# Destination one-hots of a step by two operations of a tensor with a tensor in place of eight with a per-partition scalar

## The chip, the cores and the metric

The kernel runs on one core of one Trainium2 chip. The metric is the device time of one execution in microseconds (us), the median of the runs shown. Engines: PE is TensorE, DVE is VectorE, ACT is ScalarE, POOL is GpSimd, SP is SyncE.

## What is computed

A graph layer with a residual and a layer norm over 12,500 nodes with 32 features and 200,000 edges, sorted by destination. For each edge from `src` to `dst`:

```python
msg = jnp.concatenate([x_i, x_j - x_i], axis=-1)   # x_i = x[dst], x_j = x[src]
h = relu(msg @ W1 + b1)      # 64 -> 64
h = relu(h @ W2 + b2)        # 64 -> 128
h = relu(h @ W3 + b3)        # 128 -> 64
m = h @ W4 + b4              # 64 -> 32
s = segment_sum(m, dst); cnt = segment_sum(1, dst)
x = layernorm(x + s / maximum(cnt, 1))
```

The edge attributes take no part in it. W4 is applied after the sum over the edges of a node.

## The kernel before

The edges are handled in 196 steps of 1,024 edges (`PT` = 8 tiles of 128). A step comes in one of two kinds, which `STEPS` and `SORTED_AT` lay out by hand: 60 are "sorted" (the rows of the source nodes are selected by matmuls with one-hots that DVE builds) and 136 are "gathered" (the rows are fetched by indirect DMAs that POOL issues). From step 7 to step 188 every third step, at four places every fourth, is a sorted one; the last seven steps are gathered ones.

POOL has one job in the steps: `gather(g)`, whose L585 issues one indirect DMA for each tile of a gathered step, eight to a step, 1,083 in all. They fill a ring `xj` of `R` = 10 steps; `gather` waits (`s_turned`) only if the ring is full.

PE runs the pipeline of a step: the source rows (for a gathered step L919 transposes them out of `xj`; for a sorted one `selected_x`, L964, works in three pieces spread over this and the two preceding steps, and L978 applies layer 1), the destination part of layer 1 (L901), layer 2 (L988), layer 3 (L996), the transposition of its output (`turn_layer3`, L1004), and `sum_window`, which multiplies by the one-hots of the destinations and so sums over the edges (L1016 for a sorted step, 84 nodes wide, L1019 for a gathered one, 42 wide). ACT does the ReLUs.

DVE works through `step(s)` in an order written out by hand. After `copy_x` (L1389) and `copy_layer3(s - 3)` (L1395) come:

- `build_pick(s + 1)`: one comparison of 126x1024 16-bit integers (L1367, for a sorted step L1365, and then `build_wide_pick`, L1371, as a second one);
- `build_onehot(s - 3, tiles)`: for each of the eight tiles one operation of `iota` with a scalar of each partition from `dst_rel` (L1410), float32, 42 columns for a gathered step and 84 for a sorted one, into `onehot`, which is float32 too;
- `hot_of(s, n)`: up to three comparisons of about 128x1500 16-bit integers (`build_hot`, L1380), the one-hots of the sources of the coming sorted steps, eight for each sorted step;
- `add_sums(s - 4)`: adds the sums of a step out of PSUM to `sums` (L1433), one addition for a sorted step and two for a gathered one, each at an offset that is read from memory.

The eight operations of `build_onehot` are made in four pairs with the comparisons between them:

```python
build_pick(s + 1); onehot_free(s - 3)
build_onehot(s - 3, (0, 1))
if next step is sorted: build_wide_pick(s + 1)
build_onehot(s - 3, (2, 3)); hot_of(s, 0)
build_onehot(s - 3, (4, 5)); hot_of(s, 1)
build_onehot(s - 3, (6, 7)); add_sums(s - 4)
hot_of(s, 2)
```

`onehot_free` waits for PE's sum of two steps before, `build_hot` for the landing of its row of sources and, on the first chunk of a piece, for PE; the others of these operations have no wait ahead of them. The steps 3 to 6 (`early_step`) use `build_whole_onehot` (L1418), one operation of a tensor with a tensor for all eight tiles, 336 columns. Before the steps, DVE sorts keys (`merge`: L1290 and L1291, both inputs in SBUF) and splits rows (L1162, both inputs in SBUF), while POOL already issues gathers. After the last step, `messages` (L1081) and the layer norm follow.

Of the kernel before, what the change touches and what calls it, by code (L numbers as in the profile page):

```python
# [9 lines left out]
ALU = mybir.AluOpType  # L10
# [6 lines left out]
P = 128  # L17
# [5 lines left out]
PT = 2 * UT  # L23
PE2 = PT * T
S_N = -(-E // PE2)
# [88 lines left out]
def build(nc, x, src, dst, W1, b1, W2, b2, W3, b3, W4, b4, consts, bounds, out):  # L114
# [3 lines left out]
    with ctx:  # L118
        def sb(name, shape, dt):
            return ctx.enter_context(nc.sbuf_tensor(name, shape, dt))  # L120

        def sem(name):
            return ctx.enter_context(nc.semaphore(name))

        def part(v, first, shape):
            cols = 1
            for n in shape:
                cols *= n
            names = "abcd"[:len(shape)]
            return v[:, first:first + cols].rearrange(  # L130
                f"p ({' '.join(names)}) -> p {' '.join(names)}", **dict(zip(names, shape)))
# [38 lines left out]
        onehot = part(region, 0, (2, PT, WIN))  # L170
# [20 lines left out]
        dst_rel = sb("dst_rel", [P, S_N * PT], F32)  # L191
# [107 lines left out]
        s_pick, s_oh, s_h3c, s_acc = sem("pick_built"), sem("onehot_built"), sem("layer3_copied"), sem("sums_added")  # L299
# [14 lines left out]
        def is_sorted(s):  # L314
            return STEPS[s] < SB
# [788 lines left out]
        def _(dve):  # L1104
# [160 lines left out]
            while size <= PE2:  # L1265
                j = size // 2
# [103 lines left out]
            def build_wide_pick(s):  # L1370
                nc.vector.tensor_scalar(pick[:, s % 2, 1, :], dstb[:, s % RX, :], node_off[0:K3, 2:3], None, ALU.is_equal)\  # L1371
                    .then_inc(s_pick, 1)
# [30 lines left out]
                if s == 0:  # L1403
                    dve.wait_ge(s_dst_st, 2 * 16)

            def build_onehot(s, tiles):
                v, n = s % 2, STEPS[s]
                nodes, w = (iota_s, WIN) if n < SB else (iota_g, KN)
                for j in tiles:
                    last = nc.vector.tensor_scalar(onehot[:, v, j, 0:w], nodes[:, :],  # L1410
                                                   dst_rel[:, n * PT + j:n * PT + j + 1], None, ALU.is_equal)
                if j == PT - 1:
                    last.then_inc(s_oh, 1)

            def build_whole_onehot(s):
                v, n = s % 2, STEPS[s]
# [25 lines left out]
            def hot_of(s, n):  # L1442
                for lead in (1, 2, 3):
                    if s >= AHEAD and s + lead < S_N and is_sorted(s + lead) and n < len(PIECES[3 - lead]):
                        build_hot(STEPS[s + lead], PIECES[3 - lead][n])
# [14 lines left out]
            def step(s):  # L1460
                if s < AHEAD + 3:
                    early_step(s)
                    return
                if s < S_N and is_sorted(s):
                    copy_x(s)
                if s <= S_N + 2:
                    copy_layer3(s - 3)
                if s + 1 < S_N:
                    build_pick(s + 1)
                if s <= S_N + 2:  # L1470
                    onehot_free(s - 3)
                    build_onehot(s - 3, (0, 1))
                if s + 1 < S_N and is_sorted(s + 1):
                    build_wide_pick(s + 1)
                if s <= S_N + 2:
                    build_onehot(s - 3, (2, 3))
                hot_of(s, 0)
                if s <= S_N + 2:
                    build_onehot(s - 3, (4, 5))
                hot_of(s, 1)  # L1480
                if s <= S_N + 2:
                    build_onehot(s - 3, (6, 7))
                add_sums(s - 4)
                hot_of(s, 2)

            build_pick(0)
            for s in range(AHEAD):
# [66 lines left out]
            for n in range(len(CHUNKS) + LAG + 1):  # L1554
                if n > LAG:
                    variance(n - LAG - 1)
                if n < len(CHUNKS):
                    c0, w = CHUNKS[n]
# [44 lines left out]
```

## Time and profile before

| | us |
|---|---|
| median of 3 runs | 1553.71 |
| lowest and highest | 1542.68, 1553.79 |
| the profiled execution, its own time | 1556.37 |
| its span, first to last instruction | 1554.5 |
| busy PE / DVE / ACT / POOL | 1375.3 / 966.0 / 605.6 / 1168.6 |
| mean granted TensorE clock, share of full | 0.937 |

The span is what the rows below are read from; the profiled execution's own time has 1.9 us around it. Instructions of DVE overlap in the records: the next one starts some 0.08 us before the end of the one before it, so the time that one takes in a row of several is the distance from start to start.

### The profile page before, as it was taken

The numbers are of one execution on the slowest core, as the hardware profiler recorded it, in microseconds if no ns is written. First come the engines' busy times: TensorE is split into PE (matmuls) and PEld (weight loads), VectorE is DVE, ScalarE is ACT, GpSimd is POOL, SyncE is SP. The second block draws the span as 40 slices with busy tenths as digits, with TensorE's granted clock in tenths as the row PEclk, the third lists the DMA queues.
The fourth block names the chain that finished last, engine by engine and source line by source line (L and its number), as shares of the span: only waits on it lengthen the run. The fifth ranks groups of instructions, "written<-read, shape, count | busy, mean of one in ns | idle before, by whom it ended". The sixth has DMA issues, their size and how long they took to land.

```text
span 1554.5 us, 40899 instructions
## 1 busy us (share of the span) xinstructions
PE 1375.3 (88%) x14064; PEld 930.6 (60%) x14064; DVE 966.0 (62%) x3159; ACT 605.6 (39%) x952; POOL 1168.6 (75%) x1101
## 2 busy tenths in 40 slices
PE   3254999999999999999989999999899989999676
PEld 2112666666767766766756666666566656766443
DVE  5986566666666666666556666665556655666355
ACT  5354333443343443444333433434324343333323
POOL 4777777777777777777777777777777777777752
PEclk8566999999999999999999999999989998999868
DMA  7538977777767777777667777767657775775411
GB/s 183 163 88 188 296 232 228 220 223 225 226 202 233 232 225 220 224 214 228 185 176 224 209 225 215 213 201 203 196 173 233 209 217 171 233 221 158 105 30 44
DMA packets 197031, 306.55 MB, mean 197 GB/s; under 512 B 84519, under 2 KB 90010, under 8 KB 196257
## 3 DMA queue, kind: packets, MB, share of 16 engines
q1 hardware_dynamic: 161485, 267.17, 56.2%
q0 software_dynamic: 34656, 34.90, 10.5%
q8 instruction: 115, 1.88, 0.5%
q10 hardware_dynamic: 682, 1.85, 0.5%
q14 instruction: 93, 0.75, 0.2%
HBM read 289.68 MB, written 13.92 MB: 195 GB/s over the span
## 4 chain that ended last, share of the span: by engine, by line
POOL 66%; issue 20%; DVE 5%; PE 3%; DMA 3%; SPq 2%; ACT 0%; DVEq 0%; POOLq 0%; ACTq 0%
POOL xj L585 66%; DVE region L1290 1%; DVE region L1291 1%; DMA sums<-in_src 1%; SPq L524 1%; DMA x_rows<-x_p 1%; PE ps L964 1%; DMA xj<-z_rows,src_t 1%; DVE work L1156 0%; PE ps L1019 0%; PE ps L988 0%; DVE work L1162 0%; PE ps L996 0%; DMA region<-src_rows 0%; PE ps L1081 0%
## 5 line engine op out<-in xcount | busy, mean ns | idle before, releaser
L585 POOL DMA_INDIRECT xj<-z_rows,src_t x1043 | 1111.1, 1065 | 317.9 <-issue 317.0
L964 PEld LDWEIGHTS ps<-region,x_p 128*96 128x96 bf16 x6780 | 397.8, 126 | 53.8 <-issue 53.2
L964 PE MATMUL ps<-region,x_p 128*96 128x127 bf16 (+54 forms) x6780 | 418.6, 220 | 8.1 <-DVE region L1380 8.1
L731 ACT ACTIVATE work<-ps,b3s 128x512 f32<-128x512 f32 x196 | 134.7, 687 | 562.7 <-PE ps L996 554.7
L1380 DVE TENSOR_SCALAR region<-region,cst 128x1629 bf16<-128x1629 int16 x480 | 302.1, 630 | 13.3 <-DMA region<-src_rows 13.1
L1395 DVE COPY work<-ps 128x512 f32<-128x512 f32 x195 | 133.9, 687 | 271.2 <-PE ps L1004 268.9
L724 ACT ACTIVATE work<-ps,b2s 128x512 f32<-128x512 f32 x392 | 248.0, 683 | 69.8 <-PE ps L988 69.8
L716 ACT ACTIVATE work<-ps,b1s 128x512 f32<-128x512 f32 x196 | 134.7, 687 | 237.8 <-PE ps L901 237.5
L988 PE MATMUL ps<-work,w2s 64*128 64x512 f32 x784 | 224.9, 651 | 1.0 <-ACT work L716 0.9
L996 PE MATMUL ps<-work,w3s 128*64 128x512 f32 x784 | 213.3, 623 | 0.0
L1410 DVE TENSOR_SCALAR region<-iota_g,dst_rel 128x42 f32<-128x42 f32 x1056 | 206.7, 251 | 0.0
L919 PEld LDWEIGHTS ps<-cst,xj 128*128 128x128 f32 x544 | 60.2, 147 | 185.2 <-issue 185.1
L919 PE MATMUL ps<-cst,xj 128*128 128x128 f32 x544 | 93.3, 297 | 79.3 <-DMA xj<-z_rows,src_t 65.0
L988 PEld LDWEIGHTS ps<-work,w2s 64*128 64x128 f32 x784 | 59.9, 187 | 168.3 <-issue 111.9
L1019 PE MATMUL ps<-region,work 128*65 128x42 f32 x2176 | 156.2, 235 | 1.9 <-DVE sums L1433 1.9
L1019 PEld LDWEIGHTS ps<-region,work 128*65 128x65 f32 x2176 | 154.8, 145 | 3.1 <-issue 3.0
L1389 DVE CAST work<-ps 96x512 bf16<-96x512 f32 x60 | 41.2, 687 | 158.9 <-PE ps L964 153.2
L1433 DVE TENSOR_TENSOR sums<-sums,ps 65x42 f32 (+1 forms) x332 | 65.6, 198 | 108.5 <-DVE sums L1433 97.1
L1004 PE MATMUL ps<-cst,work 128*128 128x128 f32 x784 | 131.6, 292 | 0.0
L1004 PEld LDWEIGHTS ps<-cst,work 128*128 128x128 f32 x784 | 86.0, 146 | 33.9 <-issue 33.1
L1410 DVE TENSOR_SCALAR region<-iota_s,dst_rel 128x84 f32<-128x84 f32 x480 | 101.7, 268 | 0.0
L901 PE MATMUL ps<-region,ywin 126*64 126x512 bf16 x512 | 94.1, 403 | 6.4 <-DVE region L1367 6.4
(156 smaller groups left out, 810.1 us busy)
## 6 DMA issues: line engine op xcount, KB each, us to landing
dstb<-dst_rows SPq DMA_DIRECT2D x196, 252.0 KB
region<-src_rows SPq DMA_DIRECT2D x120, 391.2 KB
region<-src_rows SPq DMA_DIRECT2D x60, 407.2 KB
region<-src_rows SPq DMA_DIRECT2D x60, 403.2 KB
region<-src_rows SPq DMA_DIRECT2D x60, 376.2 KB
region<-src_rows SPq DMA_DIRECT2D x60, 375.8 KB
region<-src_rows SPq DMA_DIRECT2D x60, 374.0 KB
region<-src_rows SPq DMA_DIRECT2D x60, 366.2 KB
```

Of the source, the lines that this page charges most:

```text
L585: pool.indirect_dma_start(out=xj[:, u, j % UT, j // UT, 0:w], out_offset=None, in_=rows, in_offset=bass.IndirectOffsetOnAxis(ap=cols[:, j: ...
L716: nc.scalar.activation(h1[:, v, :], p_h1, ACT.Relu, bias=b1s[:, 0:1]).then_inc(s_r1, 1)
L724: nc.scalar.activation(h2[:, v, h, :], p_h2[:, h, :], ACT.Relu, bias=b2s[:, 0:1]).then_inc(s_r2[h], 1)
L731: nc.scalar.activation(h3[:, v, :], p_h3, ACT.Relu, bias=b3s[:, 0:1]).then_inc(s_r3, 1)
L919: turned = nc.tensor.matmul(to[:, t * T:(t + 1) * T], xj[:, u, t, :, :].rearrange("p h f -> p (h f)"), ident, start=t == 0, stop=True, is_ ...
L964: chosen = nc.tensor.matmul(ps[0:XP, XBANK[h], lo - h * UE:hi - h * UE], xb[:, a, :], hot[:, q % QN, at + lo:at + hi], start=not begun[h], ...
L988: nc.tensor.matmul(p_h2[:, h, :], w2s[r:r + H1, :], h1[r:r + H1, s % 2, :], start=True, stop=True).then_inc(s_l2[h], 1)
L996: nc.tensor.matmul(p_h3[h * H3:(h + 1) * H3, :], w3s[:, :], h2[:, s % 2, h, :], start=True, stop=True).then_inc(s_l3, 1)
L1004: turned = nc.tensor.transpose(p_ht[:, t * T:(t + 1) * T], h3[:, s % 2, t * T:(t + 1) * T], ident)
L1019: summed = nc.tensor.matmul(p_agg[:, h * KN:(h + 1) * KN], h3t[:, v, t, h, :], onehot[:, v, j, 0:KN], start=t == 0, stop=t == UT - 1)
L1380: nc.vector.tensor_scalar(hot[:, q % QN, 0:CW[c]], spread[:, q % QE, 0:CW[c]], cst[:, C_PID:C_PID + 1], None, ALU.is_equal).then_inc(s_hot, 1)
L1410: last = nc.vector.tensor_scalar(onehot[:, v, j, 0:w], nodes[:, :], dst_rel[:, n * PT + j:n * PT + j + 1], None, ALU.is_equal)
```

## The change

`build_onehot` makes half of the tiles of a step in one operation of a tensor with a tensor, in which both inputs are spread by a stride of zero, so that two operations stand in place of eight. Their places among the comparisons change with it.

```diff
-            def build_onehot(s, tiles):
+            def build_onehot(s, j0, j1):
                 v, n = s % 2, STEPS[s]
                 nodes, w = (iota_s, WIN) if n < SB else (iota_g, KN)
-                for j in tiles:
-                    last = nc.vector.tensor_scalar(onehot[:, v, j, 0:w], nodes[:, :],
-                                                   dst_rel[:, n * PT + j:n * PT + j + 1], None, ALU.is_equal)
-                if j == PT - 1:
-                    last.then_inc(s_oh, 1)
+                made = nc.vector.tensor_tensor(onehot[:, v, j0:j1, 0:w],
+                                               nodes[:, :].unsqueeze(1).to_broadcast([P, j1 - j0, w]),
+                                               dst_rel[:, n * PT + j0:n * PT + j1].unsqueeze(2).to_broadcast([P, j1 - j0, w]),
+                                               ALU.is_equal)
+                if j1 == PT:
+                    made.then_inc(s_oh, 1)
...
                 if s <= S_N + 2:
                     onehot_free(s - 3)
-                    build_onehot(s - 3, (0, 1))
+                    build_onehot(s - 3, 0, PT // 2)
                 if s + 1 < S_N and is_sorted(s + 1):
                     build_wide_pick(s + 1)
+                else:
+                    hot_of(s, 0)
                 if s <= S_N + 2:
-                    build_onehot(s - 3, (2, 3))
-                hot_of(s, 0)
-                if s <= S_N + 2:
-                    build_onehot(s - 3, (4, 5))
-                hot_of(s, 1)
-                if s <= S_N + 2:
-                    build_onehot(s - 3, (6, 7))
+                    build_onehot(s - 3, PT // 2, PT)
+                if s + 1 < S_N and is_sorted(s + 1):
+                    hot_of(s, 0)
+                else:
+                    hot_of(s, 1)
                 add_sums(s - 4)
-                hot_of(s, 2)
+                if s + 1 < S_N and is_sorted(s + 1):
+                    hot_of(s, 1)
+                else:
+                    hot_of(s, 2)
```

## Rows read from the trace of the kernel before

**Rows 1.** The page, part 4: the chain of work that ended last, by line.
```profile
POOL xj L585 66%; DVE region L1290 1%; DVE region L1291 1%; DMA sums<-in_src 1%; SPq L524 1%; DMA x_rows<-x_p 1%; PE ps L964 1%; DMA xj<-z_rows,src_t 1%; DVE work L1156 0%; PE ps L1019 0%; PE ps L988 0%; DVE work L1162 0%; PE ps L996 0%; DMA region<-src_rows 0%; PE ps L1081 0%
```
**Rows 2.** Stretches: window, length, then PE, PEld, DVE, ACT, POOL busy (instructions), granted clock, DMA.
```profile
165.00:700.00 535.00, 535.00 (x5792) 368.24 (x5791) 349.38 (x1188) 217.16 (x346) 417.64 (x386) 1.00 0.76 227
700.00:1500.00 800.00, 737.62 (x7583) 504.51 (x7580) 466.71 (x1605) 296.47 (x466) 620.47 (x590) 0.96 0.67 195
```
**Rows 3.** Timeline of POOL, 564 to 575 us: start, length, instruction, idle before.
```profile
564.63 2.39 POOL L585 DMA_INDIRECT xj<-z_rows,src_t  x1 [0.30 <-issue]
567.33 0.94 POOL L585 DMA_INDIRECT xj<-z_rows,src_t  x1 [0.30 <-issue]
...
572.60 1.37 POOL L585 DMA_INDIRECT xj<-z_rows,src_t  x1 [0.30 <-issue]
```
**Rows 4.** Timeline of DVE, the same stretch.
```profile
564.21 0.47 DVE L1367 TENSOR_SCALAR region<-dstb,node_off 126x1024 bf16<-126x1024 int16 x1
564.60 0.78 DVE L1410 TENSOR_SCALAR region<-iota_s,dst_rel 128x84 f32<-128x84 f32 x4
565.31 0.64 DVE L1380 TENSOR_SCALAR region<-region,cst 128x1629 bf16<-128x1629 int16 x1
565.87 0.42 DVE L1410 TENSOR_SCALAR region<-iota_s,dst_rel 128x84 f32<-128x84 f32 x2
566.21 0.60 DVE L1380 TENSOR_SCALAR region<-region,cst 128x1496 bf16<-128x1496 int16 x1
...
567.07 0.19 DVE L1433 TENSOR_TENSOR sums<-sums,ps 65x42 f32 x1
...
572.54 0.60 DVE L1380 TENSOR_SCALAR region<-region,cst 128x1503 bf16<-128x1503 int16 x1
```
**Rows 5.** The chain in order of time: first and last POOL pieces like that at 564.63.
```profile
337.47 2.39 POOL xj L585
...
1358.92 2.39 POOL xj L585
```
**Rows 6.** Timeline of POOL before the steps and in the early ones.
```profile
50.65 2.83 POOL L585 DMA_INDIRECT xj<-in_x,src_t  x1 [0.30 <-issue]
...
163.13 1.17 POOL L585 DMA_INDIRECT xj<-z_rows,src_t  x1 [0.31 <-issue]
```
**Rows 7.** Timeline of DVE, the same stretches.
```profile
50.78 1.21 DVE L1162 TENSOR_TENSOR work<-work 125x1024 bf16<-125x1024 f32 x1
51.92 0.41 DVE L1290 TENSOR_TENSOR region<-region 128x256 f32<-128x256 f32 x1
52.25 0.41 DVE L1291 TENSOR_TENSOR region<-region 128x256 f32<-128x256 f32 x1
...
162.99 0.49 DVE L1418 TENSOR_TENSOR region<-iota_g,dst_rel 128x336 f32<-128x336 f32 x1
163.40 0.18 DVE L1433 TENSOR_TENSOR sums<-sums,ps 65x42 f32 x1
```
**Rows 8.** Groups of DVE by line and form: count, busy, mean ns, idle before.
```profile
L1410 DVE TENSOR_SCALAR region<-iota_g,dst_rel 128x42 f32<-128x42 f32 x1056 | 206.7, 251 | 0.0
L1410 DVE TENSOR_SCALAR region<-iota_s,dst_rel 128x84 f32<-128x84 f32 x480 | 101.7, 268 | 0.0
```
**Rows 9.** The page, part 5: the comparisons of the sources.
```profile
L1380 DVE TENSOR_SCALAR region<-region,cst 128x1629 bf16<-128x1629 int16 x480 | 302.1, 630 | 13.3 <-DMA region<-src_rows 13.1
```
**Rows 10.** Timeline of DVE at the end of the steps.
```profile
1522.53 1.29 DVE L1410 TENSOR_SCALAR region<-iota_g,dst_rel 128x42 f32<-128x42 f32 x8
...
1524.95 0.20 DVE L1433 TENSOR_TENSOR sums<-sums,ps 65x42 f32 x1 [0.75 <-DVE sums L1433]
```
**Rows 11.** Timeline of PE at the end of the steps.
```profile
1525.30 1.11 PE L1019 MATMUL ps<-region,work 128*65 128x42 f32 x16 [1.14 <-DVE sums L1433]
```
**Rows 12.** Timeline of DVE and of PE ahead of a sorted step.
```profile
579.64 0.19 DVE L1433 TENSOR_TENSOR sums<-sums,ps 65x42 f32 x1
581.39 0.82 PE L964 MATMUL ps<-region,x_p 128*96 128x144 bf16 x10
```

## The prediction

> **What bounds the kernel now.** I read the chain of waits first: 66% of it is L585, the issue of the gathers on POOL [rows 1]. Then the stretches. In the first, 165 to 700 us, PE is busy without a break, and in the second, up to 1500 us, it is idle for 800 - 737.62 = 62 us [rows 2]. That looks like two bounds, but POOL is the same in both: 976 gathers in 1335 us, busy 1038 us, which leaves 0.30 us between two of them, the idle time that each gather's row shows [rows 3]. POOL waits for nobody. In the first stretch PE lives on the ten steps of gathers that POOL has ahead; when these are used up, PE waits. So the end of the steps is when POOL has issued its last gather, and only a shorter gather moves it, as long as PE has idle time left: 62 us.
>
> Then the length of a gather. Undisturbed it takes 0.94 us [rows 3]; the mean is 1038/976 = 1.064 us [rows 2]. The excess over 976 x 0.94 = 917 us is 121 us, and it is what this change can touch. Where it comes from is seen when POOL's rows are laid beside DVE's. The gather of 572.60 takes 1.37 us and ends at 573.97, 0.83 us after the 16-bit comparison that began just before it, at 572.54, ends (573.14) [rows 3, 4]. A gather thus needs something near its start that DVE's operation holds, and has some 0.82 us of work left from there. The gather of 564.63 takes 2.39 us and so gets it only at about 566.2, after a pick, four one-hots, a comparison and two more one-hots, all end to end [rows 3, 4]; there are fifteen of 2.39 us or more from 337 to 1359 us [rows 5]. The gather of 567.33 comes when DVE is adding out of PSUM, and takes 0.94 us [rows 3, 4].
>
> **The change part by part.** What matters is for how long DVE holds what a gather needs, and how the holding operations stand end to end.
>
> Held now, by distance from start to start: a one-hot of 42 columns takes (1.29 - 0.25)/7 = 0.15 us [rows 8, 10], one of 84 columns (565.31 - 564.60)/4 = 0.18 us [rows 4], a comparison 0.63 - 0.08 = 0.55 us [rows 4, 9], a pick 0.39 us [rows 4]. With 1056, 480 and 480 of the first three [rows 8, 9] and 256 picks (196, and 60 wide ones): 158 + 86 + 264 + 100 = 608 us, 45% of the stretches' 1335 us. The excess is 121/608 = 0.20 us for each us held.
>
> Removed are the 1536 small operations, 244 us of it. Added are 264 operations of 128x168 (132 gathered steps) and 120 of 128x336 (60 sorted ones). The form is in the trace: L1418, 128x336, takes 0.49 us and the next begins 0.41 us after it; L1290 with 256 columns takes 0.41 us [rows 7]. That is 0.001 us a column, so 168 columns take 0.32 us, 0.24 from start to start. Sum: 264 x 0.24 + 120 x 0.41 = 63 + 49 = 112 us. On DVE itself the change is a gain of 132 us, which moves nothing in the steps, since DVE is busy for 816 of 1335 us and is released by PE.
>
> Does the new operation hold a gather too? It has both inputs in SBUF. The gather of 163.13 takes 1.17 us and ends 0.82 us after L1418 ends (163.48), not after the addition behind it; the gather of 50.65 takes 2.83 us and ends 0.82 us after L1291 ends (52.66), behind three such operations end to end [rows 6, 7]. So it does, for as long as it runs. The bounds of this term: it holds as a small one-hot does, us for us, or not at all; I take the first, by these two gathers.
>
> Held after: 608 - 244 + 112 = 476 us. The 15 long stalls cost 15 x 1.45 = 22 us; the other 99 us of excess shrink with what is held: 99 x 132/608 = 21 us less.
>
> The long stalls depend on the row of operations end to end. In the row from 564.21 to 567.07 [rows 4] there are eleven (one pick, eight one-hots, two comparisons), with ten joints at which a gather can lose its turn again; after the change there are five, with four joints, and the row is 0.39 + 0.41 + 0.56 + 0.41 + 0.52 = 2.3 us long in place of 2.9. Between no gain and 22 us I take half, 11 us.
>
> The moved comparisons. In a gathered step without a sorted one next, the first comparison comes behind one operation of 0.24 us in place of four of 0.15, so earlier. In the step ahead of a sorted one the last comparison falls behind both additions: before, the first addition was at 579.64 and PE began the selection that needs it at 581.39 [rows 12]. By the lengths above, the additions now start 1.2 us earlier (0.7 us of one-hots, 0.5 us of comparison), take 1.1 us with the address read between them, and the comparison ends near 580.1: 1.3 us before PE asks. It costs nothing; were that cover gone, each of the 60 sorted steps would pay at most 0.6 us. The load of the next row of sources is issued by SP some 0.7 us later than now, steps ahead of its use.
>
> The end of the steps. There, no gathers are left, and PE waits up to 1.14 us for DVE's addition, which stands behind eight one-hots of 1.29 us [rows 10, 11]. Two operations take 0.56 us. The addition then waits for PE's own sum instead, so of 0.7 us in each of two or three steps I count 1 us in all (none to 2).
>
> Sum: 21 + 11 + 1 = 33 us off the profiled execution's 1556.4 us. The median of the runs is 2.7 us below that execution, so 1553.7 - 33 = 1521 us. PE's 62 us of idle time cover it.
>
> **The rivals.** *The new operation does not hold a gather.* The page "SBUF — State Buffer" of the Trainium skill, section "Who interferes with whom", says that an operation with two SBUF inputs takes only the shared read interface, and infers that issuing a DMA from POOL needs the write one, so that it would not be stalled; the same section says that it does contend with whatever POOL reads. By the first of these the two gathers of rows 6 should not have been long; by the second they should. As a mechanism of this kernel: held after is 608 - 244 = 364 us, the excess falls by 99 x 244/608 = 40 us, each new operation breaks a row, so that the 22 us of long stalls go, and with the end's 1 us the sum is 63 us, where PE's idle time of 62 us also ends it: 1491 us. Against it stand the two gathers.
>
> *The hits move on and nothing is won.* The gathers come every 1.25 us and DVE's rows are some 3 us long, so both run in step: a stall at the same place comes back again and again [rows 5]. What a gather now loses to one-hots it may lose to the 16-bit comparisons, 0.55 us each, behind which it can be kept through the new operation of 0.24 to 0.41 us as well, where it was kept through one small one of 0.15. With all 121 us of excess kept, the time is 1553 us; with half of the gain, 1537.
>
> *Slower: gathers are kept through the whole new row.* The place is the row of a step from its first new operation to the second: 0.24 + 0.55 + 0.24 = 1.03 us (1.37 in a sorted step). Three operations of this kind end to end kept the gather of 50.65 for 1.9 us [rows 6, 7], which small one-hots do only fifteen times in 1335 us. If one gather of a step is caught so, the price is 1.1 us, against the 33 us won; it decides from 30 of the 185 steps on. With 60 of them: 66 - 33 = 33 us more, 1587 us. For it speaks that DVE's steps repeat in time; against it, that the comparison between the two waits for its load's semaphore, and that L1418's gather was let in right behind it [rows 7].
>
> **How the numbers follow.** Forecast 0.58, no hold 0.10, nothing won 0.22, slower 0.10. About 1% (15.5 us) is what a measurement of this kernel can tell from no change. Faster by over 1% takes the no-hold case, nearly all of the forecast's, and a little of the third with half of the gain: 0.67. Within 1%: 0.24. Slower: 0.09. The range leaves out the slower case and half of the no-hold one: 1494 to 1551 us.
>
> **What would show it.** In the profile after, L1410 is gone; two operations stand in a step, near 0.32 us (128x168) and 0.49 us (128x336). DVE's busy time falls by about 130 us or more. The mean of L585 falls from 1.065 to about 1.035 us and its idle time between two stays 0.30 us. Fewer gathers of over 2 us. PE's idle time in the steps falls from 62 to about 30 us. The time from the last gather to the end changes by 1 us. Wrong would be: a mean of L585 that stays, with the same count of long ones; gathers that end 0.82 us after a second new operation in most steps; a gather of 0.94 us that starts under a new operation throughout; POOL waiting on PE.

## The result, and the profile after

| | before | after |
|---|---|---|
| median, us | 1553.75 | 1573.97 |
| lowest and highest of 4 | 1542.68, 1554.44 | 1571.73, 1584.55 |
| span of the profiled execution | 1554.5 | 1582.7 |
| busy DVE / POOL | 966.0 / 1168.6 | 836.1 / 1199.4 |
| gathers that fall in 165 to 700 us | 386 | 375 |
| gathers over 1.8 us, 165 to 1501 us, counted in the trace | 18 | 46 |

The kernel became slower: ratio 1.0171 [1.0103, 1.0238], 20 us. The forecast was 1521 us and its range ended at 1551. The profiled execution is the slowest of the four, so the traces lie 28 us apart; two more executions of the kernel after took 1571.47 and 1589.94 us.

The page of the kernel after, part 1 (engines), part 4 (the chain by engine) and two rows of part 5 (count, busy us and mean ns, idle time before and its releaser):

```profile
PE 1386.7 (88%) x14064; PEld 943.9 (60%) x14064; DVE 836.1 (53%) x2007; ACT 606.2 (38%) x952; POOL 1199.4 (76%) x1101
...
POOL 72%; issue 21%; DVE 2%; DMA 2%; PE 2%; ACT 0%; DVEq 0%; SPq 0%; POOLq 0%; ACTq 0%
...
L585 POOL DMA_INDIRECT xj<-z_rows,src_t x1043 | 1141.7, 1095 | 318.2 <-issue 317.5
...
L1409 DVE TENSOR_TENSOR region<-iota_g,dst_rel 128x168 f32<-128x168 f32 x264 | 84.8, 324 | 0.0
```

The groups of POOL by line, kernel before; this row of L585 is what the one above answers to:

```profile
L585 POOL DMA_INDIRECT xj<-z_rows,src_t x1043 | 1111.1, 1065 | 317.9 <-issue 317.0 <-PE ps L919 0.6 <-DMA xj<-z_rows,src_t 0.3
```

DVE does what it was meant to, 130 us less work. The chain is POOL's, more than before (72% against the 66% of L585 in [rows 1]). The same 1043 gathers are busy for 30.6 us more, and the span is 28.2 us longer. Idle time between gathers is unchanged. So the loss is in the length of the gathers alone. The windows of the kernel after, with the columns of [rows 2], say where it is:

```profile
165.00:700.00 535.00, 529.06 (x5666) 363.34 (x5665) 291.16 (x706) 214.03 (x340) 420.90 (x375) 0.99 0.75 223
700.00:1500.00 800.00, 743.89 (x7616) 513.38 (x7613) 389.35 (x945) 294.96 (x464) 624.11 (x577) 0.95 0.68 196
```

Eleven gathers fewer in the first window and thirteen fewer in the second. PE, busy without a break there before, now has 6 us of idle time in the first window already.

POOL's timeline of the kernel after answers to [rows 3]; its two long gathers are one period of the steps apart:

```profile
565.19 1.25 POOL L585 DMA_INDIRECT xj<-z_rows,src_t  x1 [0.30 <-issue]
566.74 2.31 POOL L585 DMA_INDIRECT xj<-z_rows,src_t  x1 [0.30 <-issue]
...
586.99 2.30 POOL L585 DMA_INDIRECT xj<-z_rows,src_t  x1 [0.30 <-issue]
```

DVE's timeline beside it answers to [rows 4]:

```profile
565.84 0.47 DVE L1367 TENSOR_SCALAR region<-dstb,node_off 126x1024 bf16<-126x1024 int16 x1
566.24 0.50 DVE L1409 TENSOR_TENSOR region<-iota_s,dst_rel 128x336 f32<-128x336 f32 x1
566.66 0.64 DVE L1380 TENSOR_SCALAR region<-region,cst 128x1629 bf16<-128x1629 int16 x1
567.21 0.49 DVE L1409 TENSOR_TENSOR region<-iota_s,dst_rel 128x336 f32<-128x336 f32 x1
567.63 0.60 DVE L1380 TENSOR_SCALAR region<-region,cst 128x1496 bf16<-128x1496 int16 x1
568.15 0.18 DVE L1434 TENSOR_TENSOR sums<-sums,ps 65x42 f32 x1
```

From here on "to keep a gather" means that DVE's work makes it take longer than undisturbed, and the "row" is the operations of DVE that stand end to end. The gather of 566.74 ends at 569.05, which is 0.82 us after the second comparison ends (567.63 + 0.60 = 568.23). It met the first comparison and was kept through that, the one-hot of 336 columns and the next comparison, to the point where DVE goes on to add out of PSUM. That is 1.36 us for one gather. Read the same way, 36 gathers in the trace are kept over exactly this row, in the one-hots of sorted steps, 1.34 us each on average.

The gather ahead of it shows a second way of being kept. That of 565.19 ends at 566.44, 0.13 us after the pick of 565.84 ends (566.31), though the pick began 0.65 us after the gather did. Of the 951 gathers of the kernel after from 165 to 1501 us, 549 take less than 0.97 us. Of the other 402, 294 end 0.82 us after a comparison, a pick or a new one-hot, 107 end 0.12 us after a comparison or a pick (all within 0.02 us), and one does neither. So a gather can be kept at two points: near its start, with 0.82 us left to do, and later, with 0.12 us left. A gather that ends less than 0.8 us after an operation was let in ahead of it.

### The profile page after: what moved, and what is told of

It reads as the page before. It is cut to its first block, busy times and chain, and to the rows that moved or that the text cites. A ratio compares the mean times of both kernels' runs of the same rounds, so it can differ in the third digit from the quotient of the medians.

```text
span 1582.7 us, 39747 instructions
## 1 busy us (share of the span) xinstructions
PE 1386.7 (88%) x14064; PEld 943.9 (60%) x14064; DVE 836.1 (53%) x2007; ACT 606.2 (38%) x952; POOL 1199.4 (76%) x1101
## 4 chain that ended last, share of the span: by engine, by line
POOL 72%; issue 21%; DVE 2%; DMA 2%; PE 2%; ACT 0%; DVEq 0%; SPq 0%; POOLq 0%; ACTq 0%
POOL xj L585 72%; DMA sums<-in_src 1%; PE ps L1019 0%; DMA xj<-z_rows,src_t 0%; DVE region L1291 0%; DVE region L1290 0%; DVE work L1156 0%; DMA z_rows<-work 0%; PE ps L850 0%; DVEq L1432 0%; DMA work<-sums 0%; DVE work L1162 0%; POOL region L617 0%; PE ps L996 0%; PE ps L829 0%
## 5 line engine op out<-in xcount | busy, mean ns | idle before, releaser
L585 POOL DMA_INDIRECT xj<-z_rows,src_t x1043 | 1141.7, 1095 | 318.2 <-issue 317.5
L964 PEld LDWEIGHTS ps<-region,x_p 128*96 128x96 bf16 x6780 | 404.9, 128 | 57.2 <-issue 56.2
L964 PE MATMUL ps<-region,x_p 128*96 128x127 bf16 (+54 forms) x6780 | 425.7, 222 | 11.4 <-DVE region L1380 11.4
L1395 DVE COPY work<-ps 128x512 f32<-128x512 f32 x195 | 134.0, 687 | 374.1 <-PE ps L1004 374.1
L1019 PEld LDWEIGHTS ps<-region,work 128*65 128x65 f32 x2176 | 158.3, 148 | 3.1 <-issue 3.0
L1409 DVE TENSOR_TENSOR region<-iota_g,dst_rel 128x168 f32<-128x168 f32 x264 | 84.8, 324 | 0.0
L1016 PE MATMUL ps<-region,work 128*65 128x84 f32 x960 | 79.4, 236 | 0.0
```

Of the source, the lines that this page charges most:

```text
L585: pool.indirect_dma_start(out=xj[:, u, j % UT, j // UT, 0:w], out_offset=None, in_=rows, in_offset=bass.IndirectOffsetOnAxis(ap=cols[:, j: ...
L964: chosen = nc.tensor.matmul(ps[0:XP, XBANK[h], lo - h * UE:hi - h * UE], xb[:, a, :], hot[:, q % QN, at + lo:at + hi], start=not begun[h], ...
L1019: summed = nc.tensor.matmul(p_agg[:, h * KN:(h + 1) * KN], h3t[:, v, t, h, :], onehot[:, v, j, 0:KN], start=t == 0, stop=t == UT - 1)
L1395: nc.vector.tensor_copy(h3t[:, s % 2, :, :, 0:H3], p_ht.rearrange("p (t h f) -> p t h f", t=UT, h=2))\
```

## The experiments

All 15 kernels compute the same result; some carry an extra wait or memset, as their edit shows. The figures first, in the order of the runs. The ratio is to the kernel before on the same chip, with its interval. L585 busy and the gathers that fall in 165 to 700 us are from the profile, and the last two columns are counted in the trace, 165 to 1501 us (excess is time over that run's own undisturbed gather, 0.944 to 0.947 us). Compare the ratios and not the medians: the kernel before took 1559.4 us beside e1 to e4, 1552.9 beside e5 to e8 and 1556.2 beside the others.

| run | median us | ratio | L585 busy | 165 to 700 | over 1.8 us | excess us |
|---|---|---|---|---|---|---|
| before | 1553.75 | 1 | 1111.1 | 386 | 18 | 118 |
| after | 1573.97 | 1.0171 [1.0103, 1.0238] | 1141.7 | 375 | 46 | 144 |
| e1 | 1552.07 | 0.9959 [0.9932, 0.9987] | - | - | - | - |
| e2 | 1593.11 | 1.0223 [1.0181, 1.0266] | 1146.9 | 375 | 52 | 154 |
| e3 | 1579.42 | 1.0124 [1.0083, 1.0165] | 1136.2 | 375 | 45 | 142 |
| e4 | 1523.96 | 0.9774 [0.9733, 0.9816] | 1079.2 | 398 | 0 | 86 |
| e5 | 1592.59 | 1.0253 [1.0215, 1.0291] | 1151.4 | 375 | 93 | 158 |
| e6 | 1530.64 | 0.9854 [0.9818, 0.989] | 1090.7 | 396 | 28 | 99 |
| e7 | 1603.79 | 1.0329 [1.0289, 1.0369] | 1157.9 | 376 | 52 | 164 |
| e8 | 1536.85 | 0.9905 [0.9873, 0.9938] | 1093.2 | 396 | 17 | 101 |
| e9 | 1584.78 | 1.0188 [1.0137, 1.0239] | 1133.7 | 377 | 38 | 140 |
| e10 | 1582.25 | 1.0156 [1.0102, 1.0211] | 1136.9 | 378 | 45 | 144 |
| e11 | 1558.01 | 0.9996 [0.9973, 1.0018] | 1109.8 | 386 | 15 | 117 |
| e12 | 1580.92 | 1.0143 [1.0091, 1.0195] | 1139.5 | 378 | 42 | 144 |
| e13 | 1581.18 | 1.0161 [1.0114, 1.0209] | 1140.9 | 376 | 45 | 146 |
| e14 | 1581.88 | 1.016 [1.012, 1.0199] | 1141.1 | 374 | 46 | 147 |
| e15 | 1540.26 | 0.9892 [0.9856, 0.9928] | 1099.6 | 389 | 25 | 107.5 |

Edits are against the kernel after unless it says otherwise.

### e1: the new order with the old operations

```diff
-                made = nc.vector.tensor_tensor(onehot[:, v, j0:j1, 0:w],
...
+                for j in range(j0, j1):
+                    made = nc.vector.tensor_scalar(onehot[:, v, j, 0:w], nodes[:, :],
+                                                   dst_rel[:, n * PT + j:n * PT + j + 1], None, ALU.is_equal)
```

> The order of the change with the eight operations with a scalar of before (four, a comparison, four, a comparison, the addition). Theory A: in the row of a sorted step's one-hots a gather that arrives in the first comparison is kept through the 336-column operation and the next comparison (36 such gathers of the changed kernel, 1.36 us each), so that operation is needed: here near the kernel before, 0.99 to 1.01 of it, few gathers over 2 us between comparison and comparison. Theory B: two SBUF inputs in one operation keep a gather, whatever its size and place: also 0.99 to 1.01. Theory C: the new places of the comparisons do it, not the operations: 1.01 to 1.02, mean gather near 1.095 us.

It takes 1552.07 us, 0.9959 [0.9932, 0.9987]. The order of the comparisons is not the cause. The profiled execution of this kernel was disturbed (5213 us), so nothing is read from its trace.

### e2: the new operations in the old order

Against the kernel before: four operations of two tiles each, where the four pairs stood.

```diff
-                    build_onehot(s - 3, (0, 1))
+                    build_onehot(s - 3, 0, 2)
...
-                    build_onehot(s - 3, (2, 3))
+                    build_onehot(s - 3, 2, 4)
```

> The order of before, each pair of tiles made by one operation of a tensor with a tensor (84 or 168 columns, four to a step). Theory A: no operation of 336 columns, so no stall through comparison, one-hot, comparison: 0.98 to 1.00 of before. Theory B: twice as many operations with two SBUF inputs as in the changed kernel: 1.01 to 1.03. Theory C: the old order, so 0.99 to 1.00.

1.0223 [1.0181, 1.0266]. With e1 this is the crossed pair: old operations in the new order lose nothing, new operations in the old order lose as much as the change. It is the kind of operation, and not its length, as the widest is 168 columns here.

### e3: no operation wider than 168 columns

```diff
+                k = 2 if n < SB else 4
+                for j in range(j0, j1, k):
+                    made = nc.vector.tensor_tensor(onehot[:, v, j:j + k, 0:w],
```

> The changed kernel, but a half of a sorted step is made by two operations of 128x168 in place of one of 128x336; gathered steps as changed. Theory A: the long stalls behind the first comparison go: 1525 to 1550 us, 0.98 to 1.00 of before. Theory B: more such operations: 1.015 to 1.03. Theory C: the order stays, so 1.01 to 1.02.

1.0124 [1.0083, 1.0165], 45 long gathers in place of 46. With e2 this ends the theory that the 336 columns are what keeps a gather.

### e4: one input in PSUM

`iota` is copied once into free columns of a PSUM bank, and the one-hots read it there. A wait for PE's sums of an earlier step comes with it, as PE writes that bank.

```diff
+        p_iota_s, p_iota_g = ps[:, 6, 256:256 + WIN], ps[:, 6, 384:384 + KN]
...
-                nodes, w = (iota_s, WIN) if n < SB else (iota_g, KN)
+                nodes, w = (p_iota_s, WIN) if n < SB else (p_iota_g, KN)
...
+                    dve.wait_ge(s_agg, s - 3)
```

> The changed kernel, but the node numbers that the one-hots are compared with lie in PSUM (copied there once), so that each of the two operations has one input in SBUF; before the first of them DVE also waits for PE's sum of the step before, whose bank holds them. Theories A and B: one-hots keep no gather and break the rows, excess per gather from 0.15 to under 0.08 us, 1490 to 1535 us, 0.96 to 0.99 of before. Theory C: no change against the changed kernel, 1.01 to 1.02.

1523.96 us, 0.9774 [0.9733, 0.9816]: the fastest kernel of the study, ahead of both. Its timelines of POOL and DVE:

```profile
566.59 1.60 POOL L586 DMA_INDIRECT xj<-z_rows,src_t  x1 [0.30 <-issue]
568.50 0.95 POOL L586 DMA_INDIRECT xj<-z_rows,src_t  x1 [0.30 <-issue]
...
586.83 1.60 POOL L586 DMA_INDIRECT xj<-z_rows,src_t  x1 [0.30 <-issue]
```

```profile
566.08 0.50 DVE L1410 TENSOR_TENSOR region<-ps,dst_rel 128x336 f32<-128x336 f32 x1
566.50 0.64 DVE L1381 TENSOR_SCALAR region<-region,cst 128x1629 bf16<-128x1629 int16 x1
567.05 0.49 DVE L1410 TENSOR_TENSOR region<-ps,dst_rel 128x336 f32<-128x336 f32 x1
567.47 0.60 DVE L1381 TENSOR_SCALAR region<-region,cst 128x1496 bf16<-128x1496 int16 x1
567.99 0.19 DVE L1435 TENSOR_TENSOR sums<-sums,ps 65x42 f32 x1
```

The row is that of the kernel after, to 0.01 us, and the gather comes at nearly the same place, 0.09 us after the first comparison begins (0.08 there). But it takes 1.60 us, not 2.31. It ends at 568.19, 0.12 us after the second comparison ends (568.07), so it was let in ahead of that comparison and then kept by it at its second point. In this trace 27 gathers met the first comparison of such a row, and all 27 end so.

The one-hots alone show the difference too. Two gathers that begin 0.13 and 0.14 us into a one-hot of 168 columns, first POOL's and DVE's row of the kernel after:

```profile
182.97 1.00 POOL L585 DMA_INDIRECT xj<-z_rows,src_t  x1 [0.30 <-issue]
```

```profile
182.84 0.32 DVE L1409 TENSOR_TENSOR region<-iota_g,dst_rel 128x168 f32<-128x168 f32 x1
```

and those of e4:

```profile
182.81 0.94 POOL L586 DMA_INDIRECT xj<-z_rows,src_t  x1 [0.30 <-issue]
```

```profile
182.67 0.31 DVE L1410 TENSOR_TENSOR region<-ps,dst_rel 128x168 f32<-128x168 f32 x1
```

With both inputs in SBUF the gather ends at 183.97, 0.81 us behind the one-hot (183.16); with one in PSUM it is not kept. Of the gathers that begin 0.03 to 0.14 us into a new one-hot, of either width, 60 of 60 end 0.82 us behind it in the kernel after, and none of 52 in e4: 27 take at most 0.954 us, and 25 end 0.12 us after the comparison that follows. So the operation with one input in PSUM keeps no gather; with both in SBUF it does. This fits the Trainium skill, "SBUF — State Buffer", section "Who interferes with whom", where an operation of DVE with at most one SBUF input, outside the fast modes, leaves POOL's ports alone.

### e5: the additions ahead of the comparison

```diff
                     build_onehot(s - 3, PT // 2, PT)
+                add_sums(s - 4)
...
-                add_sums(s - 4)
```

> The changed kernel with add_sums moved ahead of the comparison that follows the second one-hot operation, so that the row of operations that keep a gather ends at that operation. Theory D (after the first four runs: a gather is not let in at the joints between a comparison and an operation of a tensor with a tensor, in whatever width, and waits for the end of the row): the stalls that start in the first comparison shrink from 1.36 to about 0.85 us, some 18 us less than the changed kernel, 1550 to 1562 us. If the number of such operations alone counted (theory B): no change, 1570 to 1580 us.

1.0253 [1.0215, 1.0291]: slower than the change, where 1550 to 1562 us was expected. The addition shortens the row, but it puts two comparisons end to end behind it. In the trace 46 gathers are kept there for 0.89 us each, and 27 are still kept 1.40 us, most of them from the pick at the head of the row on, where the kernel after has only a few. The miss shows that comparison on comparison keeps a gather too.

### e6 and e7: one kind of step at a time

e6 uses the old operations in the 60 sorted steps and the new ones in the gathered steps; e7 is the reverse (`n >= SB`).

```diff
+                if n < SB:
+                    for j in range(j0, j1):
+                        made = nc.vector.tensor_scalar(onehot[:, v, j, 0:w], nodes[:, :],
...
+                else:
+                    made = nc.vector.tensor_tensor(onehot[:, v, j0:j1, 0:w],
```

> The changed kernel, but the 60 sorted steps' one-hots are made by eight operations with a scalar again (four, comparison, four); gathered steps as changed. Theory D: the 36 long stalls all lie in the rows of sorted steps' one-hots, and joints with a small one-hot let a gather in, so they go: 1530 to 1550 us. Theory B: 264 of the 384 new operations are left, so most of the loss stays: 1565 to 1575 us.

> The changed kernel, but the gathered steps' one-hots are made by eight operations with a scalar again; the 60 sorted steps as changed. Theory D: the rows with the long stalls are kept: 1565 to 1585 us. Theory B: a third of the new operations is left: 1555 to 1565 us.

e6 takes 1530.64 us, 0.9854 [0.9818, 0.989]; e7 1603.79 us, 1.0329 [1.0289, 1.0369]. The windows of the first stretch, L585 of POOL alone (length, busy and instructions, clock, DMA share, GB/s), of e6:

```profile
165.00:700.00 535.00, 414.59 (x396) 1.00 0.78 228
```

and of e7:

```profile
165.00:700.00 535.00, 420.65 (x376) 0.99 0.75 222
```

This divides the change in two. In the gathered steps it is a gain of 1.5%, where the forecast wanted 2.1% from all steps; in the 60 sorted ones it is a loss of over 3%, more than the 1565 to 1585 us expected. The two add up to the change (-0.0146 + 0.0329 = +0.0183 against +0.0171), but e15 shows that such sums fail elsewhere.

### e8 and e11: the wait of e4 alone

```diff
                     onehot_free(s - 3)
+                    dve.wait_ge(s_agg, s - 3)
```

> Control for the run with the node numbers in PSUM: the changed kernel with its added wait alone (DVE waits for PE's sum of the step before ahead of the first one-hot operation), inputs in SBUF. If the gain there came from the inputs: as the changed kernel, 1568 to 1580 us. If the wait, by a pause in the row behind the pick, gave it: 1525 to 1545 us.

> The kernel before with the wait of the control run alone (DVE waits for PE's sum of the step before ahead of the first one-hot). Theory L: the time moves without any change of the operations, by 5 to 25 us in either direction, as the count in the first stretch leaves 385. If only operations with two SBUF inputs are sensitive to it: within 0.5% of before.

e8, on the kernel after: 1536.85 us, 0.9905 [0.9873, 0.9938]. e11, the same line in the kernel before: 0.9996 [0.9973, 1.0018], nothing. It is no new wait: `add_sums(s - 4)` makes the same one further down in the same step, and here it stands ahead of the one-hots. So the wait has no worth of its own, but most of e4's gain comes with it: the busy time of L585 goes from 1141.7 us (the change) to 1093.2 (e8) to 1079.2 (e4), so 48.5 us of it are there without PSUM and 14.0 us are what the inputs in PSUM add. No run has them without the wait. The timeline of POOL in e8 shows another rhythm:

```profile
559.36 1.10 POOL L585 DMA_INDIRECT xj<-z_rows,src_t  x1 [0.30 <-issue]
...
567.51 1.23 POOL L585 DMA_INDIRECT xj<-z_rows,src_t  x1 [0.30 <-issue]
569.04 1.18 POOL L585 DMA_INDIRECT xj<-z_rows,src_t  x1 [0.30 <-issue]
...
579.60 1.10 POOL L585 DMA_INDIRECT xj<-z_rows,src_t  x1 [0.30 <-issue]
```

And DVE's timeline of e8 in the sorted step:

```profile
567.03 0.47 DVE L1367 TENSOR_SCALAR region<-dstb,node_off 126x1024 bf16<-126x1024 int16 x1
567.42 0.50 DVE L1409 TENSOR_TENSOR region<-iota_s,dst_rel 128x336 f32<-128x336 f32 x1
567.84 0.64 DVE L1380 TENSOR_SCALAR region<-region,cst 128x1629 bf16<-128x1629 int16 x1
568.39 0.49 DVE L1409 TENSOR_TENSOR region<-iota_s,dst_rel 128x336 f32<-128x336 f32 x1
568.81 0.60 DVE L1380 TENSOR_SCALAR region<-region,cst 128x1496 bf16<-128x1496 int16 x1
```

Fifteen gathers lie between 559.36 and 579.60, and none comes in the first comparison. One meets the first one-hot and is let in at its end (567.92), the next meets the second comparison. The row of operations is the same; most gathers miss its costly place. The 14 in the trace that do begin in the first comparison are all kept to the end of the second, 1.28 us each, against 36 in the kernel after. So the wait does not open the row; only in e4 is it open. Why the wait moves the gathers, I can't say. What it does to DVE in this trace is a pause of some 0.2 us between pick and one-hot in about 50 of the gathered steps.

### e9, e10: the row of the sorted steps moved

A memset of 340 (e10: 130) columns ahead of the sorted step's one-hots, to move the row later against the gathers.

```diff
+                    if is_sorted(s - 3):
+                        nc.vector.memset(x_t[:, :, :, :].rearrange("p a t n -> p (a t n)")[:, 0:340], 0.0)
```

> The changed kernel with a memset of 340 columns on DVE (about 0.4 us, it reads nothing) ahead of the one-hots of the 60 sorted steps, so that their row comes 0.4 us later than the gathers that meet it. Theory L (the gathers' 1.25 us and DVE's 20.24 us period from PE are locked: a whole number of gathers, 14 or 15, falls into the period, and the excess is what is left over; where the lock falls depends on fine positions): with more work on DVE the time moves by more than 10 us, most likely down, 1525 to 1560 us, with near 395 gathers from 165 to 700 us in place of 375. Theory D alone (the row of operations decides, not its position): 1570 to 1585 us.

> The same with 130 columns (about 0.2 us). Theory L: again a whole or half number of gathers in a period, 375, 385 or 395 in the first stretch, and a time that need not lie between those of no memset and of 340 columns. Theory D alone: 1570 to 1585 us.

1.0188 [1.0137, 1.0239] and 1.0156 [1.0102, 1.0211]: 38 and 45 long gathers. The theory that the row only happens to lie badly falls, and with it the forecast that such a push moves the time by over 10 us. The gathers follow the row.

### e12: the gathers moved instead

```diff
+                if g >= R + 2:
+                    nc.gpsimd.memset(x_t[0:1, 0, 0, g - R - 2:g - R - 1], 0.0)
```

> The changed kernel with one memset of a single element on POOL, some 0.1 us, ahead of the eight gathers of each of 124 gathered steps, 12 to 20 us of work in all on the engine that bounds the kernel. Without a lock it adds: 1586 to 1596 us. Theory L: in the first stretch the excess takes it up (the count stays 374 or 375, the mean gather falls) or the lock changes to 15 gathers and the time falls by over 10 us; in no case is the addition simply seen.

The groups of POOL by line in this run:

```profile
L587 POOL DMA_INDIRECT xj<-z_rows,src_t x1043 | 1139.5, 1093 | 300.0 <-issue 299.2 <-DMA xj<-z_rows,src_t 0.6
...
L585 POOL MEMSET x_t<- 1x1 f32 x124 | 24.2, 195 | 0.0
```

The memsets take 24.2 us and the idle time between gathers falls by 18, so POOL gets 6 us more to do and the gathers' time falls by 2 us. The ratio, 1.0143 [1.0091, 1.0195], can't be told from the change's. Too small a push to decide anything.

### e13, e14: a break behind each sorted one-hot

A memset of 130 (e14: 16) columns behind each of the two operations of a sorted step.

```diff
+                if n < SB:
+                    nc.vector.memset(x_t[:, :, :, :].rearrange("p a t n -> p (a t n)")[:, (2 * n + (j1 == PT)) % 6 * 140:(2 * n + (j1 == PT)) % 6 * 140 + 130], 0.0)
```

> The changed kernel with a memset of 130 columns (about 0.2 us on DVE, it reads nothing) right behind each of the two one-hot operations of the 60 sorted steps: 24 us more work on DVE, but the row comparison, one-hots, comparison is broken. Theory D (a gather waits to the end of a row of operations that keep it): the gathers kept for 1.36 us get in behind the second one-hot operation at the latest, near 0.8 us, and the time falls under the changed kernel's by 15 to 45 us, 1530 to 1560 us. If the two-input operations cost the gathers by their number alone: 1570 to 1585 us.

> The same with memsets of 16 columns, under 0.1 us. Theory D, if an operation that keeps no gather is enough however short: as the run with 130 columns, 1530 to 1560 us. If a real pause is needed: as the changed kernel, 1570 to 1580 us.

1.0161 [1.0114, 1.0209] and 1.016 [1.012, 1.0199]: no different from the change. POOL's and DVE's timelines of e13:

```profile
504.57 2.35 POOL L585 DMA_INDIRECT xj<-z_rows,src_t  x1 [0.30 <-issue]
```

```profile
504.62 0.52 DVE L1380 TENSOR_SCALAR region<-region,cst 128x1629 bf16<-128x1629 int16 x1
505.06 0.49 DVE L1409 TENSOR_TENSOR region<-iota_s,dst_rel 128x336 f32<-128x336 f32 x1
505.53 0.17 DVE L1416 MEMSET x_t<- 128x130 f32 x1
505.61 0.49 DVE L1380 TENSOR_SCALAR region<-region,cst 128x1496 bf16<-128x1496 int16 x1
```

The gather ends at 506.92, 0.82 us after the second comparison (506.10). It sat through a memset of 0.17 us, which has no input at all, and was not let in. So it is not enough that some short operation stands between the holding ones; this ended my explanation of e6 by "breaks". But the memset overlaps its neighbours: only 0.06 us lie between the end of the one-hot (505.55) and the start of the comparison (505.61), and in e14 the memset's record lies wholly under that of the comparison. A real pause was not tried.

### e15: both repairs together

The old operations in the sorted steps, as in e6, and the wait of e8.

> The gathered steps as changed, the sorted steps with eight scalars, and the wait of the control run: each of the two alone took the changed kernel from 1574 to 1531 and to 1537 us. Both have 15 gathers in each 20.24 us already, so they should not add: 1520 to 1540 us. If the effects were additive: under 1515 us.

0.9892 [0.9856, 0.9928]: no better than e6 (0.9854) or e8 (0.9905) alone. The repairs don't add up. That fits gathers that lock at one place or another, and not a price for each operation; 389 gathers in the first stretch are between the 396 of e6 and of e8 alone and the 386 of the kernel before.

## Why the prediction was wrong

**Right: the bound.** Span less busy time of L585 is 1554.5 - 1111.1 = 443.4 us before and 1582.7 - 1141.7 = 441.0 after; over all the profiles here but e1's it lies between 440.4 and 444.2. The time is the length of the gathers plus a constant. The issue gap stayed 0.30 us. The page of e4 names PE for 52% of its chain, but only because semaphores of PE fall into POOL's ordinary gaps: no gap ahead of a gather is over 0.32 us from 165 us on, in e4 or in any other of these profiles.

**Right: the lengths.** L1409 takes 0.324 us with 168 columns; with 336 it is this row of the groups by line, kernel after:

```profile
L1409 DVE TENSOR_TENSOR region<-iota_s,dst_rel 128x336 f32<-128x336 f32 x120 | 59.3, 497 | 0.0
```

Forecast were 0.32 and 0.49 us, and DVE's busy time was to fall by about 130 us (966.0 - 836.1 = 129.9).

**Right in part: the hold.** The new operation does keep a gather, as the two gathers of [rows 6] said: 60 of 60 in the kernel after (see e4). The inference in the Trainium skill, "SBUF — State Buffer", section "Who interferes with whom", that an operation with two SBUF inputs doesn't stall the issue of a DMA from POOL, is contradicted by it, and by e4, where the same row with one input in PSUM costs the gather 0.71 us less. Where that page and these traces differ, the traces decide; the no-hold rival falls.

**Wrong: "it holds as a small one-hot does, us for us".** The difference is at the joints with the comparisons. These are the gathers that begin while the first of the two comparisons of a sorted step's row runs (1629 columns, the second 1496), and how many of them are kept at least to the end of the second:

| run | between the two comparisons | met the first | kept to the end of the second |
|---|---|---|---|
| before | two with a scalar | 9 | 0 |
| e6 | four with a scalar | 29 | 0 |
| e15 | four with a scalar, and the wait | 14 | 0 |
| after | one of 336 columns, inputs in SBUF | 36 | 36 |
| e7 | the same | 30 | 30 |
| e8 | the same, and the wait | 14 | 14 |
| e3 | two of 168, inputs in SBUF | 36 | 36 |
| e2 | one of 168, inputs in SBUF | 9 | 9 |
| e4 | one of 336, one input in PSUM, and the wait | 27 | 0 |

Yet two SBUF inputs between two comparisons are not the whole condition. In the gathered steps of the kernel after the same kinds of operation stand in the same order, with 168 columns between two comparisons of 1565, and there all 52 gathers that met the first were let in ahead of the second. POOL's and DVE's timelines of one:

```profile
203.33 1.25 POOL L585 DMA_INDIRECT xj<-z_rows,src_t  x1 [0.30 <-issue]
```

```profile
203.05 0.62 DVE L1380 TENSOR_SCALAR region<-region,cst 128x1565 bf16<-128x1565 int16 x1
203.59 0.32 DVE L1409 TENSOR_TENSOR region<-iota_g,dst_rel 128x168 f32<-128x168 f32 x1
203.83 0.63 DVE L1380 TENSOR_SCALAR region<-region,cst 128x1565 bf16<-128x1565 int16 x1
```

It ends at 204.58, 0.12 us after the second comparison (204.46), so it had been let in before. Width does not explain it, as 168 columns are enough in e2 and e3. In the few gathered steps whose comparisons are the sorted step's, 1629 and 1496 columns, the operation of 168 columns kept 2 of 3 gathers in the kernel after and 3 of 6 in e10. What closes the joints of the sorted step, the comparisons' own lengths or the layout of the one-hots (84 columns a tile, 42 in a gathered step), no run isolates.

**Right: the moved comparison costs nothing.** DVE's last comparison ahead of a sorted step and PE's selection, kernel after:

```profile
581.21 0.59 DVE L1380 TENSOR_SCALAR region<-region,cst 128x1465 bf16<-128x1465 int16 x1
```

```profile
583.02 1.72 PE L964 MATMUL ps<-region,x_p 128*96 128x144 bf16 x29
```

It ends at 581.80, 1.2 us ahead of PE; forecast were 1.3.

**Wrong, small: the end of the steps.** Forecast was 1 us. The two one-hots are short there, but the steps keep their distance, 3.15 us, as before:

```profile
1552.16 0.19 DVE L1434 TENSOR_TENSOR sums<-sums,ps 65x42 f32 x1 [0.92 <-PE ps L1019]
1555.31 0.20 DVE L1434 TENSOR_TENSOR sums<-sums,ps 65x42 f32 x1 [0.92 <-PE ps L1019]
```

DVE now waits 0.92 us for PE's sum. In these last steps nothing is won. The whole stretch from the last gather's end to the end of the span did go from 48.2 to 45.3 us, but it lies anywhere between 45.3 and 48.6 in the other runs, at 45.4 in e9 and 48.3 in e10, which differ in the width of a memset alone. So no run shows that as the work of the change.

**Wrong: "the other 99 us of excess shrink with what is held".** Held time fell by the 132 us worked out, 22%, and the excess rose, as counted in the traces, from 118 to 144 us, where the prediction read 121 before. It is no average over DVE's busy time. Nor is a gather kept at one place only, as the prediction read from [rows 3, 4]: 107 of the 402 that are kept in the kernel after end 0.12 us after a comparison or a pick. POOL's gathers come every 1.25 us, and while PE sets the pace DVE's rows repeat every 20.24 us; the two run in step. In the first stretch of the kernel after, 14 gathers go into a period, and in e8 15. The same point of the row meets the same gather, period after period. Two rows of POOL's timeline, kernel after, one such period, fourteen gathers from the first to the second:

```profile
506.02 2.31 POOL L585 DMA_INDIRECT xj<-z_rows,src_t  x1 [0.31 <-issue]
...
526.26 2.31 POOL L585 DMA_INDIRECT xj<-z_rows,src_t  x1 [0.30 <-issue]
```

PE's timeline has the same period:

```profile
505.13 0.84 PE L978 MATMUL ps<-work,w1p 96*64 96x512 bf16 x6
...
525.37 0.84 PE L978 MATMUL ps<-work,w1p 96*64 96x512 bf16 x6
```

With 0.944 + 0.304 us for an undisturbed gather and its gap, 14 leave 20.24 - 14 x 1.248 = 2.77 us of excess in a period and 15 leave 1.52. The kernel before lies between the two (386 gathers in 26.4 periods is 14.6). The kernel after is at 14 nearly throughout (375 is 14.2), and so are all the slow kernels, 374 to 378; e4, e6 and e8 are at 15 (396 to 398).

**Wrong: "between no gain and 22 us I take half", the long stalls.** I took fewer joints for fewer chances to be kept. What decided is whether a gather meets the one place where it is kept long: the first comparison of a sorted step, with a two-input operation and a comparison behind it. There 36 gathers lose 48 us together, where the kernel before had 18 long gathers in all. The sign of this term was wrong, and it is larger than all the others: 11 us of gain were forecast.

**The rival that came.** The slower one, "gathers are kept through the whole new row", named the row and priced it at 1.1 us for each gather, deciding from 30 steps on; 1.36 us and 36 gathers were measured. What spoke against it was that L1418's gather was let in right behind it [rows 7]. But behind L1418 stood an addition out of PSUM, not a comparison. One gather in front of another neighbour was read as a rule. The rival was itself too wide: in the gathered steps of the kernel after no gather is kept through such a row between comparisons of 1565 columns. It was given 0.10.

**Shown and still open.** Shown: the kind of operation (e1 with e2), not its width (e2, e3) and not the order (e1); in the sorted steps (e6, e7); through the second SBUF input, on that row (e4 with e8, 0 of 27 against 14 of 14). Argued only: that the counts of 14 and 15 gathers in a period are a lock, and that e8 wins by its moving; the timeline of e8 is in accord with it, but e9, e10 and e12 did not move it when pushed. Open: at which joint of a row a waiting gather is let in, since the same order of operations lets it in in gathered steps and not in sorted ones, a memset without a pause does not do it (e13) and an additional comparison keeps it as well (e5); and why a wait that is hardly felt helps the new operations (e8) and not the old ones (e11).

## What to carry to other kernels

Where POOL issues DMAs without a break and sets the time, the length of its instructions is what is to be watched, and DVE's busy time is no measure of it: look at which operation of DVE stands behind the one that a gather meets. An operation of a tensor with a tensor that takes over from one with a scalar per partition is cheaper for DVE and may be dearer for POOL; try it with one input in PSUM, and in one kind of step at a time. Do not scale a gain or a loss by the busy time: where two engines are periodic, as here, it may come in whole gathers per period.

## What I had not expected of the hardware

- The time is the gathers' busy time plus 440.4 to 444.2 us in every kernel here, from e4 with 1079.2 us to e7 with 1157.9.
- The count of gathers in a period holds against pushes: with memsets of 0.34 us (340 columns) ahead of the sorted rows, 377 gathers fit into the first stretch, against 375 without them.
- The gather waiting behind DVE isn't let in by the next operation without inputs (e13: kept over a memset of 0.17 us), yet it is let in between a comparison and a one-hot with one input in PSUM (e4: 27 of 27), and between a comparison and a one-hot of 168 columns with both in SBUF in the gathered steps (kernel after: 52 of 52).
- A gather can be kept late in its work. Some 30 gathers of the kernel after that run beside DVE's copy out of PSUM (L1395) and take 1.03 to 1.26 us look as if the copy kept them, but they end 0.12 us after the pick that follows it; other gathers that run beside this copy take 0.947 us.
- An undisturbed gather took 0.944 us before and 0.947 after, some 3 us over all of them. I have no explanation for it.
